# A decoder layer on one core: forming the feed-forward's first operands in the last batch, its second half's differences half a pass ahead, and loading the rows of the last sums set by set

## The reference

```python
x = x + attn(layernorm(x))        # 32 heads, causal, ALiBi; Wqkv, q and k normalised, Wout
x = x + xattn(layernorm(x), ctx)  # linear attention against a context of 128 rows, 8 heads
x = x + ffn(layernorm(x))         # w2 @ (silu(w1 @ x) * (w3 @ x)), hidden 2752, 4-bit weights with scales
```

## Time and profile before

| | us |
|---|---|
| median of 3 runs (3208.47 to 3210.69) | 3209.15 |
| the profiled execution: its own time | 3206.32 |
| its span in the profile | 3204.5 |
| PE busy | 3013.5 (94%) |
| DVE busy | 1809.7 (56%) |
| ACT busy | 1178.9 (37%) |
| POOL busy | 902.4 (28%) |

### The profile page before, as it was taken

One profiled execution on the slowest core, in us unless ns is written; L12 is line 12 of the kernel. 1 busy time (PEld: TensorE's weight loads), 2 busy tenths in 40 slices (PEclk: granted clock), 3 DMA queues, 4 the chain that ended last, 5 costly groups with the idle time before them and its releaser, 6 DMA issues. The chain is left out here.

```text
span 3204.5 us, 40225 instructions
## 1 busy us (share of the span) xinstructions
PE 3013.5 (94%) x14656; PEld 2300.6 (72%) x14656; DVE 1809.7 (56%) x2939; ACT 1178.9 (37%) x2618; POOL 902.4 (28%) x775
## 2 busy tenths in 40 slices
PE   7999999699999999999999779999899999999999
PEld 6888888466666666666666468888688888788887
DVE  5311111466666666666666676666866666454543
ACT  2100000456556666666665333333333333111110
POOL 2100000233343333334333333333233332221221
PEclk9999999799999999999999889999999999999999
DMA  4222222201111111111111223222432235633323
GB/s 143 94 76 73 71 73 73 101 28 47 46 46 53 52 46 47 51 46 50 55 46 40 95 71 97 96 86 79 136 114 86 86 93 164 174 98 100 94 64 118
DMA packets 103341, 256.88 MB, mean 80 GB/s; under 512 B 12352, under 2 KB 18496, under 8 KB 101184
## 3 DMA queue, kind: packets, MB, share of 16 engines
q1 hardware_dynamic: 103232, 255.39, 24.8%
HBM read 181.95 MB, written 73.40 MB: 80 GB/s over the span
## 5 line engine op out<-in xcount | busy, mean ns | idle before, releaser
L1685 PE MATMUL ff_room<-xy,ring 128*128 128x512 f32 x1860 | 444.7, 390 | 7.7 <-PEq L924 7.2
L1685 PEld LDWEIGHTS ff_room<-xy,ring 128*128 128x128 f32 x1860 | 350.1, 188 | 82.6 <-issue 9.7
L1685 PE MATMUL ff_room<-xz,ring 128*128 128x512 f32 x1512 | 369.7, 394 | 20.4 <-ACT ends L1441 13.3
L1685 PEld LDWEIGHTS ff_room<-xz,ring 128*128 128x128 f32 x1512 | 288.0, 191 | 82.2 <-issue 17.3
L294 DVE TENSOR_SCALAR qkv_out<-qkv_acc 128x512 f32<-128x512 f32 x96 | 66.4, 692 | 394.9 <-PE qkv_acc L324 394.9
L1580 DVE TENSOR_TENSOR acc<-ff_room,acc 128x512 f32<-128x512 f32 x192 | 130.5, 690 | 221.9 <-PE ff_room L324 221.9
L727 ACT ACTIVATE scores<-scores,neg_max 128x128 f32<-128x128 f32 x512 | 199.1, 390 | 133.9 <-DVE neg_max L508 133.9
L1544 DVE TENSOR_TENSOR ends<-ends,ff_room 128x512 f32<-128x512 f32 x168 | 115.4, 687 | 204.6 <-ACT ends L1441 190.8
L1441 ACT ACTIVATE ends<-ff_room 128x512 f32<-128x512 f32 x126 | 75.4, 598 | 394.7 <-PE ff_room L1685 394.7
L1418 POOL TENSOR_TENSOR h_lo<-hraw,h_hi 128x2048 fp32r<-128x2048 f32 (+1 forms) x24 | 102.5, 4269 | 382.7 <-ACT h_hi L1475 382.7
L774 POOL TENSOR_TENSOR scores<-scores,row_rec 128x512 f32<-128x512 f32 x128 | 133.1, 1040 | 267.9 <-DVE row_rec L846 267.9
(11 more groups left out here) (182 smaller groups left out, 5809.2 us busy)
## 6 DMA issues: line engine op xcount, KB each, us to landing
words<-in_w SPq DMA_DIRECT2D x86, 512.0 KB, 5.0
qkv<-qkv_out SPq DMA_DIRECT2D x96, 256.0 KB, 2.0
hid<-ends SPq DMA_DIRECT2D x88, 256.0 KB, 3.3
hraw<-hid SPq DMA_DIRECT2D x20, 1024.0 KB, 5.1
qk_in<-qkv SPq DMA_DIRECT2D x16, 1024.0 KB, 4.9
w_stage<-in_w_attn SPq DMA_DIRECT2D x56, 256.0 KB, 3.1
words<-in_w SPq DMA_DIRECT2D x88, 128.0 KB, 3.8
sc<-in_s SPq DMA_DIRECT2D x44, 256.0 KB, 4.2
```

Source lines behind the costliest of these rows:

```text
L1685: last = nc.tensor.matmul(out.rearrange("p (a b) -> p a b", a=SETS), l, r, start=not onto and n == 0, stop=n == len(pairs) - 1, skip_group ...
```

## The change

It has four parts.

*Entry.* `enter_sync` (the shift amounts, the words of tile 0, the four quarters of the first half, the words of tile 1: 23 DMAs) moves on SP from turn 16 to turn 15, behind the wait for `b_done`, the last batch's context. On VectorE `unpack13(0)` moves to turn 15 behind z (`enter_vector` part 0), `difference1` behind the first residual (part 1), `difference2` ahead of the second residual (part 2). In turn 16 part 3 has the low parts of b11, A11, t1 and t2 with `difference4` and `difference3`, part 4 the low parts of S1 and of b21, part 5 at the turn's end is `unpack13(1)`; before, this one came in the first tile behind the last low part. On ScalarE the high parts of t2 and S1 move ahead of the drain's evictions of y.

*Differences.* VectorE forms t1 to t4 of the second half during the first half: in the tiles 4, 8, 12 and 16 (`PAIRS`) SP loads two rows of `xt` (`load_pair`), VectorE makes four differences of 128 by 512 behind the tile's gate (`differences`), and SP stores them to a new DRAM tensor `xd` two tiles later (`store_pair`). At the half's start SP loads R11, t1, t2, R21, R22, t3, t4 (`load_right`, `load_difference`: 28 DMAs of 256 KB; before 16), and the four large differences in tile 22 are gone. `right_high` then waits for the loads. t4 goes to R11's place and waits for R11's low part. In tile 22 the order on ScalarE and VectorE is closer; `unpack13(23)` comes ahead of the last low part.

*Sums' rows.* Ahead of the down product's loop SP now loads rows 6 and 7 alone. Sets 2 and 3 (8 to 11, 12 to 15) come behind `load2` and `load_hidden` of the steps 0 and 1.

*Semaphores.* The four pieces of the last weights in the attention's start share one semaphore, for which ScalarE waits once.

```diff
     def turn_sync(sp, b, own, cross, ahead, post):
-        if not own:
-            sp.wait_ge(s["x_done"], 2 * NB)
-            sp.wait_ge(s["xt_stored"], HALF * 16)
-            enter_sync(sp)
...
+        if own and not ahead:
+            sp.wait_ge(s["b_done"], NB)
+            sp.wait_ge(s["xt_stored"], HALF * 16)
+            enter_sync(sp)
...
     def turn_scalar(act, b, own, cross, ahead, post):
         if not own:
+            act.wait_ge(s["x_done"], 2 * NB)
             enter_scalar(act, 0)
...
     def turn_vector(dve, b, own, cross, ahead, post):
             last.then_inc(s["z_out"], 1)
+            if not ahead:
+                enter_vector(dve, 0)
...
         if own:
             residual(0)
+            if not ahead:
+                enter_vector(dve, 1)
         if not own:
-            enter_vector(dve, 0)
+            dve.wait_ge(s["x_done"], 2 * NB)
+            enter_vector(dve, 3)
         if cross:
...
+        if own and not ahead:
+            enter_vector(dve, 2)
         if not own:
-            enter_vector(dve, 1)
+            enter_vector(dve, 4)
...
         if not own:
-            enter_vector(dve, 2)
+            enter_vector(dve, 5)
...
             act.wait_ge(s["w_in"], W_PIECES * 16)
             for n in range(W_PIECES):
-                act.wait_ge(s[f"w_in{n}"], 16)
...
+    pair = place("pair", [P, 2, D], F32, 190 * KB)
+    diff = place("diff", [P, 4, N], F32, 198 * KB)
...
+    def load_difference(sp, n):
+        at, done = ((0, d_in[0]), (1, d_in[1]), (R12, r_in[R12 - R21]), (R11, r_in[R11 - R21]))[n]
+        for j in range(SETS):
+            sp.dma_start(raw[:, at, j * N:(j + 1) * N], xd[j, :, n, :]).then_inc(done, 16)
...
     def enter_vector(dve, part):
         if part == 0:
             dve.wait_ge(s["shifts"], 16)
             unpack13(dve, 0)
-            difference1(dve, 0)
+        elif part == 1:
+            difference1(dve)
+        elif part == 2:
+            difference2(dve)
+        elif part == 3:
+            right_low(dve, 0, 0)
             left_low(dve, 0, A11)
-            right_low(dve, 0, 0)
             right_low(dve, 0, 1)
-            difference2(dve, 0)
-        elif part == 1:
-            difference4(dve, 0)
+            difference4(dve)
             right_low(dve, 0, 2)
+            difference3(dve)
+        elif part == 4:
+            left_low(dve, 0, S1)
+            right_low(dve, 0, 3)
         else:
-            left_low(dve, 0, S1)
-            difference3(dve, 0)
+            unpack13(dve, 1)
...
+                def load_pair(j):
+                    if j:
+                        sp.wait_ge(s["pair_diff"], 4 * j)
+                    for i in range(2):
+                        sp.dma_start(pair[:, i, :].rearrange("p (k n) -> p k n", k=KT),
+                                     xt[HALF + i * SETS + j, :, :, :]).then_inc(s["pair_in"], 16)
+                def store_pair(j):
+                    sp.wait_ge(s["pair_diff"], 4 * (j + 1))
+                    sp.dma_start(xd[j, :, :, :], diff[:, :, :]).then_inc(s["pair_stored"], 16)
...
                     if u == 3:
                         finish_sync(sp)
+                    if u == 4:
+                        finished(sp)
+                    if u in PAIRS:
+                        load_pair(PAIRS.index(u))
+                    if u - 2 in PAIRS:
+                        store_pair(PAIRS.index(u - 2))
                     if u == WHOLE:
-                        finished(sp)
+                        sp.wait_ge(s["pair_stored"], SETS * 16)
                         sp.wait_ge(s["ab_done"], base(WHOLE))
                         load_right(sp, 1, R11)
-                        load_right(sp, 1, R12)
+                        load_difference(sp, 0)
                     store(u - 1)
                     if u == WHOLE:
+                        load_difference(sp, 1)
+                        load_right(sp, 1, R21)
                         load_right(sp, 1, R22)
-                        load_right(sp, 1, R21)
+                        load_difference(sp, 2)
+                        sp.wait_ge(s["x_lo"], OPS + 1)
+                        load_difference(sp, 3)
...
-                for t in range(6, 10):
-                    load_acc(t)
+                load_acc(6)
+                load_acc(7)
                 load_hidden(1)
-                for parity in range(2):
-                    sp.wait_ge(h_stored[parity], stored_before(TILES, parity))
-                for t in range(10, NB):
-                    load_acc(t)
                 for m in range(CHUNKS2 * SETS):
                     if 4 + m < NT:
                         load2(4 + m)
                     if 2 <= m + 2 < CHUNKS2 * SETS:
                         load_hidden(m + 2)
+                    if m == 0:
+                        for parity in range(2):
+                            sp.wait_ge(h_stored[parity], stored_before(TILES, parity))
+                    if m < 2:
+                        for t in range(SETS):
+                            load_acc((m + 2) * SETS + t)
...
+                def differences(j):
+                    b11, b21 = pair[:, 0, 0:N], pair[:, 0, N:D]
+                    b12, b22 = pair[:, 1, 0:N], pair[:, 1, N:D]
+                    dve.wait_ge(s["pair_in"], 32 * (j + 1))
+                    if j:
+                        dve.wait_ge(s["pair_stored"], 16 * j)
+                    nc.vector.tensor_tensor(diff[:, 0, :], b12, b11, ALU.subtract).then_inc(s["pair_diff"], 1)
...
                     elif u == NT:
-                        difference1(dve, 1)
                         right_low(dve, 1, 0)
+                        right_low(dve, 1, 1)
                         gate_merged(WHOLE, 0)
-                        right_low(dve, 1, 1)
-                        difference2(dve, 1)
-                        gate_merged(WHOLE, 1)
-                        difference4(dve, 1)
                         right_low(dve, 1, 2)
                         right_low(dve, 1, 3)
-                        difference3(dve, 1)
+                        gate_merged(WHOLE, 1)
                         right_low(dve, 1, 4)
                         right_low(dve, 1, 5)
+                    if u:
+                        unpack13(dve, v)
+                    if u == NT:
                         right_low(dve, 1, 6)
-                    unpack13(dve, v)
...
                     gate(u)
+                    if u in PAIRS:
+                        differences(PAIRS.index(u))
```

66 lines of the change are left out of this document (40 added, 26 removed).

## The result

The changed kernel takes 3188.01 us (median of 4 runs, 3187.86 to 3189.51) where the kernel before took 3209.92 in the runs beside it (4 runs, 3208.47 to 3212.07): 21.9 us less, a ratio of 0.9932 (95% interval 0.9915 to 0.9949). The interval excludes no change: it is faster. The forecast was 3189.0.

The account below looks back on a forecast made before the run. TensorE was taken to bound the kernel, busy 94%, so only its gaps could give time. Entry -1.9, second half -8.6 and down product -9.7 gave -20.2: 3186.1 profiled, plus 2.8 for the median, 3189.0 us; range 3182 to 3199.

Parts of the forecast that it names:

- The entry: Feed-forward start: first product 3.5 us later, A22 of tile 0 5.4 us sooner behind it; -1.9 us.
- difference2: VectorE, turn 15: it holds the last batch's second residual, which the drain inherits; +2.1 us.
- the slow A22: Tile 0 at the entry: A22's slow start, 4.12 us for 10 of its 12 rows, left as it is.
- The first half: Tiles 4, 8, 12, 16: four differences, 2.8 us, end inside VectorE's 3.46 us wait; any loss reaches TensorE a tile later.
- The second half: Tile 22: earlier operands and `unpack13(23)` bring A22 to 2303.7 instead of 2312.27; -8.6 us, bounds -4 and -11.
- rival B: Second half becomes bound by its loads, 28 DMAs at 299 GB/s: -4 us there, 3193.6 in all; chance 0.15.
- The down product: Row 4's words come earlier: the 7.54 us gap and 2.2 of the slow product behind it go; -9.7 us.
- C: Entry: drain +6 us, A22 gains 3, so +3 instead of -1.9; 3193.9 in all; chance 0.11.
- D: Row 5's words delay step 1, down product gains nothing, half only -4: -5.9 us, 3203.3, no tellable change; chance 0.04.
- E: Slower: `xd` read in 2 KB pieces delays tile 23's words at the half; 3232 at 60 GB/s; chance 0.03.
- The sum: Whole kernel: -1.9 - 8.6 - 9.7 = -20.2 us against the profiled 3206.3, giving 3186.1; median forecast 3189.0.

Follow-up runs that it names:

- the half alone: Kernel before the change with only `xd`, the pairs, the order around tile 22 and the shared semaphore changed: 3199.07 us, ratio 0.9974.
- the run with the earlier snap: Changed kernel with ScalarE's third snap of tiles 0 and 22 ahead of the copies and silu it stood behind: 3176.31 us, ratio 0.9906 of before.

## Why the prediction was right

**The entry, -1.9 forecast, -2.4 in the trace, -3.0 alone.** The first product was to come 3.5 later and came 2.6 later. `difference2` holds the second residual, as said, by 1.57 instead of 2.1 (14.23 - 12.66), for the most part because `difference1` pushed `xn` by 1.9 (10.89 behind `z` against 8.98) and not by 2.3. y is late by 2.40 (60.89 - 58.49), so 0.8 came on the way to it, and 0.6 was forecast for the copies ahead of it. That is luck in part, for two errors cancel: b11's copy started 50.50 behind `z` (48.16 before), 0.8 later than the residual alone makes it, where the forecast had it 0.5 sooner; and POOL's sums, put at 2.2 in VectorE's way, took 0.9 (3.15 for 2.28), as they were nearly done. `unpack13(1)` with POOL's addition was to cost 0.8 more than `difference3` did, and cost 0.2. Behind it, A22 was to stand 21.8 us after the first product and stands 21.34, the gap of 3.7 is 3.06. What the forecast left as it was, the slow A22, was mis-sized: 5.46 and 6.06 behind it instead of 4.58 and 5.63, 1.3 us given back in this trace.

On `difference2`, the trace and the runs together show more than the term says: putting it behind the drain's last normalisation gained nothing, as POOL's sums run there. That is the row of 4.43 for 2.29 in the earlier trace rows once more. The Trainium skill, *SBUF — State Buffer*, section *SBUF: two separate sides*, has it that a VectorE operation with two SBUF inputs and a GpSimd operation that reads SBUF exclude each other for whole instructions; the rows of 3.36 and 3.20 above, and VectorE's return to 2.28 when the sums were taken away, agree with it.

**The first half, 0 forecast, 0 measured** (381.73 with the half alone). The reason was half right. The wait that the differences fill was there. But that a loss beyond it would reach TensorE only a tile later was wrong: 6.1 us more in a tile cost 2.9 at once, by ScalarE's queue. The forecast had 4.1 us in hand without knowing it.

**The second half, -8.6 forecast, -8.4 at A22 and -7.0 at the down product.** (2304.00 against 2312.27, with the row of 60 products 0.16 later.) A11 and S1 have no gap, S3 has 1.83 (2 to 3 forecast), A22 came at 2304.00 for 2303.7. The landings were put at 2278.0, 2280.9, 2283.8, 2286.6 and 2289.5; the copies, 0.3 behind the later ones, stand at 2279.86, 2282.57, 2285.28, 2287.99 and 2290.70, so the loads came 1 to 2 us later and closer together (2.71 us each, 1.05 MB in 2.71 us is 387 GB/s). The gap before S3 is theirs. The forecast had none before S2; of the 1.36 there some 0.4 is theirs and 0.9 the first snap's place in ScalarE's queue. So rival B's cause is there, the line bounds S3, but at 365 to 394 GB/s and not at 299, and it was not worth 4 us. The forecast could have read that rate: inside the window of 364 in the earlier trace rows the trace before has 399 GB/s in 2278 to 2283. The DMA share of 1.04 and 1.05 says that all 16 engines were busy. The Trainium skill, *DMA: Bandwidth & Descriptors*, section *Measured (HBM→SBUF, 128 partitions, SWDGE, issued from GpSimd)*, has 425 GB/s for 16 MB on a core alone; the 394 measured here is near it. What was not in the sum is the clock behind the gap. A22 took 5.46 at a granted clock of 0.50, the lower of the two levels (1.2 GHz), where before it took 4.32 at 0.66; with the next product, 3.23 for 2.88, 1.5 of the 8.4 went back. In the run with the earlier snap, in which A22 has a gap of 0.47, the granted clock there is 1.00. And what the sum took over from the rows before, that sums and silu must stand ahead of the third snap, was an order of writing and no need: without it the place gave 5.9 more.

**The down product, -9.7 forecast, -9.95 measured** (479.71 against 489.66), and -10.0 in the run that changes nothing else. No gap and no slow product. The words came later than the forecast had them: row 4's were unpacked 18.9 behind the first product (13.9 forecast for their landing), row 5's 36.2 (28.2). Their second `add`s ended 2.3 and 7.3 us before TensorE asked, where the forecast had 8 and 15: the mechanism held with a small margin at row 4. All of rivals B, C, D and E missed: B by the rate, C because the drain cost 2.6 rather than 6 and A22 came 5.9 sooner behind it rather than 3, D because row 5's words still were in time, E because tile 23's words were unpacked from 2292.5 on.

**The sum, -20.2 forecast.** In the two traces it is -2.4 + 0.4 - 7.0 - 9.95 = -18.9, the 0.4 being the slow products of tile 1; with `z` 2.1 later by chance that is the -16.8 of the spans. The second trace of the changed kernel gives -19.1 in the same way. In the medians it is -21.9, and -21.5 as the sum of the parts alone. That the median came within 1.0 of the forecast is luck in part: by the traces the half gave 1.6 less, and the medians show 3.0 more than the traces, which no term of the sum explains.

## What to carry to other kernels

An engine's queue is a wait list: before a lateness is called covered, look at what stands behind the waiting instruction on each engine, for here a snap behind a copy cost 11.5 us in four places (with the differences made three times), and a snap behind a silu, in one place behind copies of the sums too, 11.6 in two. A gap of 3 to 4 us on TensorE cost up to 3 more, by the slower clock of the products behind it. Where transfers follow one another without a pause, sending one sooner only changes which of them is late.

## What the runs showed of the hardware

After a gap of 2.9 to 5.6 us the twelve products of A22 took 4.32 to 5.46 us instead of 2.88, at a granted clock of 0.66 down to 0.50; after gaps of 0.5 to 1.7 us twelve products took 3.0. At gaps of 1.83 to 1.87 it was one or the other: S3 of tile 22 took 3.0 in six traces and 4.5 to 4.6 in five, 2.99 with the half alone and 4.58 in both traces of the changed kernel, though the two do the same there. Nothing here shows what decides it.

With the queue full for longer, the line carried up to 398 GB/s over 9 us (in the run with the earlier snaps), above the 299 and 364 from which the forecast took its rates.
